# Waiting for each group of eight gathers to land before POOL issues the next

## The reference

```python
x = dense_inputs                                   # [2048, 13]
for W, b, g, be in bot:                            # 13 -> 512 -> 256 -> 64
    x = _bn(relu(x @ W + b), g, be)                # batch norm over the 2048 samples
embs = vmap(lambda tbl, idx: tbl[idx], in_axes=(0, 1), out_axes=1)(emb_tables, sparse_inputs)
T = concatenate([embs, x[:, None, :]], axis=1)     # [2048, 27, 64]
Z = einsum('bnd,bmd->bnm', T, T)                   # all pairs of the 27 vectors of a sample
h = concatenate([x, Z[:, iu, ju]], axis=1)         # 64 + 351 features
for W, b, g, be in top:                            # 415 -> 512 -> 256 -> 1
    h = _bn(relu(h @ W + b), g, be)
return sigmoid(h)
```

## Time and profile before

| | before |
|---|---|
| median of 3 runs | 589.98 us |
| lowest, highest | 588.6, 590.01 us |
| profiled execution, first to last instruction | 987.2 us |
| mean granted PE clock in it | 0.662 of full speed |
| PE, PEld, DVE, ACT, POOL busy | 448.2, 321.1, 233.0, 189.5, 401.1 us |
| gathers: L320, L331 | 390, 26 instructions |
| queue of the gathers | 13312 packets, 13.66 MB, 10.6% of 16 engines |

### The profile page before, as it was taken

One profiled execution on the slowest core, in us unless ns is written; L12 is line 12 of the kernel. 1 busy time (PEld: TensorE's weight loads), 2 busy tenths in 40 slices (PEclk: granted clock), 3 DMA queues, 4 the chain that ended last, 5 costly groups with the idle time before them and its releaser, 6 DMA issues.

```text
span 987.2 us, 13898 instructions
## 1 busy us (share of the span) xinstructions
PE 448.2 (45%) x5827; PEld 321.1 (33%) x5827; DVE 233.0 (24%) x640; ACT 189.5 (19%) x509; POOL 401.1 (41%) x426
## 2 busy tenths in 40 slices
PE   7751151624425161523517162351715244177787
PEld 3430020513214051412405051240514133165664
DVE  6600130402112040312204031220403022055542
ACT  5400020302011030302103030210303021044523
POOL 6777227072542707163361706336171634500000
PEclk9975575756657575755757575575757557577999
DMA  5122001020110202010110101011020101100000
GB/s 168 23 27 26 12 9 26 3 26 10 18 18 11 26 3 27 7 23 14 14 23 5 26 6 23 14 14 23 5 27 6 24 13 15 22 3 1 3 1 0
DMA packets 15895, 18.30 MB, mean 19 GB/s; under 512 B 7614, under 2 KB 8894, under 8 KB 15695
## 3 DMA queue, kind: packets, MB, share of 16 engines
q0 software_dynamic: 13312, 13.66, 10.6%
q1 hardware_dynamic: 2524, 3.72, 1.2%
HBM read 17.34 MB, written 0.01 MB: 18 GB/s over the span
## 4 chain that ended last, share of the span: by engine, by line
another core or an unknown queue 61%; PE 23%; ACT 10%; issue 3%; DVE 3%; DMA 0%; ACTq 0%; SPq 0%; DVEq 0%
PE l_bank L469 11%; ACT Zs L280 7%; PE l_bank L409 3%; PE l_bank L393 2%; PE l_bank L466 2%; PE l_bank L399 1%; PE l_bank L423 1%; ACT TT L636 1%; PE z_bank L455 1%; PE l_bank L507 1%; PE tr_bank L351 1%; DVE TT L853 1%; ACT hidden L582 0%; ACT hidden_hi L648 0%
## 5 line engine op out<-in xcount | busy, mean ns | idle before, releaser
L320 POOL DMA_INDIRECT emb<-table,stage x390 | 374.3, 960 | 424.1 <-DVE stage L802 309.2
L455 PE MATMUL z_bank<-TT 64*27 64x26 f32 x3840 | 127.5, 217 | 403.5 <-issue 388.4
L455 PEld LDWEIGHTS z_bank<-TT 64*27 64x27 f32 x3840 | 89.2, 132 | 442.9 <-issue 442.9
L254 DVE COPY Zs<-z_bank 27x112 f32<-27x112 f32 (+3 forms) x272 | 88.2, 324 | 498.7 <-remote 488.6
L280 ACT ACTIVATE Zs<-z_bank 27x112 f32<-27x112 f32 (+3 forms) x272 | 91.6, 337 | 552.8 <-remote 535.2
L469 PE MATMUL l_bank<-Zs,tw_sb 128*128 128x128 f32 x840 | 117.1, 298 | 0.0
L469 PEld LDWEIGHTS l_bank<-Zs,tw_sb 128*128 128x128 f32 x840 | 112.6, 215 | 0.0
L853 DVE COPY TT<-tr_bank 128x512 f32<-128x512 f32 (+1 forms) x60 | 51.1, 979 | 4.2 <-PE tr_bank L441 3.9
L351 PE MATMUL tr_bank<-idle_operand 128*128 128x512 bf16 x112 | 46.9, 590 | 0.0
L864 DVE BATCH_NORM_STATS2 stats_t<-h_block 128x128 f32 x60 | 17.7, 294 | 123.8 <-ACT hidden_hi L648 123.8
L441 PE MATMUL tr_bank<-ident,emb 128*128 128x128 f32 x195 | 30.8, 284 | 35.1 <-DVE TT L853 28.8
(11 more groups left out here) (120 smaller groups left out, 282.5 us busy)
## 6 DMA issues: line engine op xcount, KB each, us to landing
emb<-table,stage POOLq DMA_INDIRECT x416
tw_sb<-tw0x SPq DMA_DIRECT2D x1, 1792.0 KB
bw_sb<-bw SPq DMA_DIRECT2D x1, 512.0 KB
tw_sb<-tw SPq DMA_DIRECT2D x1, 512.0 KB
twx_sb<-twx SPq DMA_DIRECT2D x1, 256.0 KB
idx_raw<-idx SPq DMA_DIRECT2D x1, 169.0 KB, 3.0
bw_sb<-bw SPq DMA_DIRECT2D x2, 64.0 KB
hidden<-dense_t SPq DMA_DIRECT2D x1, 104.0 KB
```

The costliest lines, as they stand in the source:

```text
L254: last = copy(dst, src[:, :, ZC * q:ZC * q + w])
L320: pool.indirect_dma_start(out=emb[:, s, k, h, :], out_offset=None, in_=table, in_offset=bass.IndirectOffsetOnAxis(ap=stage[:, s, col:col + ...
L455: mm = nc.tensor.matmul(bank[QUAD * j:QUAD * j + V, x * ZM:(x + 1) * ZM], one, one[:, 1:V], start=True, stop=True)
```

## The change

After a group of gathers POOL waits until that group has landed, adds one to a new semaphore that nothing waits for, and then issues the next group. This happens between groups of the same part, so three times in each of parts 0 to 14. The order of the gathers, their tiles and their semaphores stay as they are. There is no wait after the last group of a part, and the gathers of part 15 are unchanged.

```diff
+        group_started = sem("group_started")
...
                     pool.wait_ge(slot_open, it * SLOTS + (s + 1))
                     pool.sem_inc(part_started, 1)
-                    for k in range(TP):
-                        for h in range(2):
-                            col = 2 * k + h
-                            pool.indirect_dma_start(
-                                out=emb[:, s, k, h, :], out_offset=None, in_=table,
-                                in_offset=bass.IndirectOffsetOnAxis(ap=stage[:, s, col:col + 1], axis=0),
-                            ).then_inc(landed[s][k // GROUP], 16)
+                    for g in range(GROUPS):
+                        if g > 0:
+                            pool.wait_ge(landed[s][g - 1], (it + 1) * (len(group_pairs(g - 1)) * 2 * 16))
+                            pool.sem_inc(group_started, 1)
+                        for k in group_pairs(g):
+                            for h in range(2):
+                                col = 2 * k + h
+                                pool.indirect_dma_start(
+                                    out=emb[:, s, k, h, :], out_offset=None, in_=table,
+                                    in_offset=bass.IndirectOffsetOnAxis(ap=stage[:, s, col:col + 1], axis=0),
+                                ).then_inc(landed[s][g], 16)
```

## The result

| | before | changed |
|---|---|---|
| median | 589.29 us | 694.59 us |
| lowest, highest | 588.0, 590.01 us (4 runs) | 694.14, 696.11 us (4 runs) |
| profiled execution, span | 987.2 us | 693.4 us |

The changed kernel is slower by 105.3 us, a ratio of 1.179 (95% interval 1.1773 to 1.1809). The forecast was 676 us with a range of 645 to 704: direction and mechanism hold, and the size of a pause was put too low.

What follows compares the result with a forecast made beforehand. The prediction took POOL's issue of gathers as the bound. Each of 45 pauses adds 1.4 + 0.81 - 0.30 = 1.9 us, 86 us together, so 590 + 86 = 676 us, with a range of 645 to 704.

Steps and rivals of the forecast that it cites:

- The bound: Timed runs are bound by POOL's issue of gathers from 4.5 to 530 us, 32.5 us a part against PE's 21.3.
- a slot open near 85: Without the crawl, the first slot for gathered data would be reopened near 85 us, against 138.98 in the trace.
- POOL is not the bound: Rival: PE sets the 590 us and pauses fill POOL's waits for a slot; time stays or falls to 530; chance 0.05.
- term (a): In each pause between groups, the last gather's data must land: 1.4 us from the end of its instruction.
- Term (b): In each pause, POOL must wake, do the increment and get the next gather going: 0.81 us.
- Term (c): The usual 0.30 us between two gathers is no longer paid by itself, so it comes off each pause.
- The high bound for (a): Landing of a group's last gather takes 1.6 us at the most from the end of its instruction.
- the sum's own high bound: 45 pauses between groups at 1.6 + 0.81 = 2.4 us, with nothing saved: 108 us, 698 us in all.
- The estimate counted from the end of the instruction: By the skill's fixed transfer cost, a pause adds 2.0 + 0.8 - 0.3 = 2.5 us: 113 us, 703 us in all.
- The late semaphores: Rival: packet records end before POOL sees the count; a pause adds 2.8 us, 126 us, 716 us in all; chance 0.07.
- the crawl of PE: PE issues only a few products at a time while POOL gathers; nearly all of it was taken to come from the recording.
- What could give time back: In the bottom network, pauses leave perhaps three fewer gathers lengthened from 0.94 to 1.4 us beside a DVE operation: -1.5 us.

Runs made afterwards that it cites:

- Runs 4 and 6: 4: kernel before with 20 more idle PE multiplies per loop part, 589.55 us; 6: kernel before with two gathers fewer in parts 0 to 14, 551.31 us.
- run 5: The kernel before, unchanged, recorded a second time: 588.51 us, recorded span 586.6 us.
- run 1: The changed kernel with each of its 45 waits and increments moved behind two gathers of the next group: 591.80 us.

## Why the prediction was right, and where it wasn't

**The bound: right.** POOL's issue sets the end. Runs 4 and 6 show it from both sides: 20 more multiplies of PE a part change about 1 us, and 30 fewer gathers give 37.2 us. The model of the chain from a disturbed recording, with the 416th gather at 529.0, a slot open near 85 and a sum of 585.5, is met by the clean recording of run 5: 529.13, 85.5 and a span of 586.6. The rival "POOL is not the bound" needed a gather of 1.07 us or less; it is 1.24.

One detail of that sum was right by luck. I took the chain through the last gather. In run 5 it leaves POOL at the 21st gather of part 15, which completes the first group of the second half:

```profile
522.89 2.72 DMA emb<-table,stage
525.61 0.04 issue
525.65 1.12 PE tr_bank L479 x4
```

PE is then busy until 532.2, when the last gather has landed anyway (530.08 + 1.78 = 531.9). Both paths end within half a microsecond of each other.

**The cost of the waits: right in kind, 0.4 us short in size.** The forecast was 86 us, measured are 105.3. The prediction's own term (a) was mis-sized. It took 1.4 us from the end of the last gather to its landing, read from the transfer engines' activity; measured is 1.78 (2.73 - 0.95). Term (b), 0.81, was measured as 0.79. Term (c), 0.30, is the one seen. The pause is then 1.78 + 0.79 - 0.30 = 2.27 us. 45 of them make 102 us. The other 3 us are pauses that are longer than the rest. The kernel's first stands beside SP's loads, and its landing comes 3.92 us after the gather's start instead of 2.73:

```profile
13.87 3.92 DMA emb<-table,stage
...
387.45 3.41 DMA emb<-table,stage
```

The first line, the kernel's first pause, is worth 1.2 us of the 3. The second line is from the loop, where SP transfers nothing; what makes its landing late isn't shown.

The high bound for (a), 1.6 us "at the most", was passed as well. That the time still lies under the 698 us of the sum's own high bound is in part luck: this bound, 1.6 + 0.81 = 2.4 us a pause, holds only because it doesn't take off the 0.30.

The rule of the Trainium skill on the fixed cost of a transfer (page "DMA: Bandwidth & Descriptors", section "Anatomy of one DMA — SWDGE (gpsimd) path": about 2 us, most of it the receipt of the write) speaks of a wait behind the data. The traces agree in kind, but they show only a quarter of a microsecond between the last recorded activity and the release of POOL, and no run tells whether the recorded activity holds more of it. The measured time is 2.7 us from the start of the gather and 1.78 from its end, and neither is 2.0. The estimate counted from the end of the instruction, 703 us, lies 8 us above the result; my sum lay 19 below.

**The late semaphores: the half of a rival that came true.** It had the count arrive after the packets, with one more idle stretch and no 0.30 taken off, 2.8 us a pause. The count does come late, by 0.25 us and not by 0.4, and the 0.30 does come off: 2.34 us a pause as timed.

**The recording: wrong.** I took the crawl of PE for something that goes with the gathers whenever this program is recorded, and expected a span near 1070 us for the changed kernel, or less if the pauses interrupt the crawl. It was 693.4, and the kernel before had 586.6 in its second recording, with the same gathers. That the crawl wasn't in the timed runs was right, and it is what the sum stood on. What caused it in one recording of eleven stays open; no run here brought it back.

**What could give time back: it did, by about 2 us.** The forecast said -1.5 us, from three fewer lengthened gathers beside the bottom network. In run 5 there are 13 gathers of 1.33 to 1.41 us up to 36 us, each with DVE's operation at L830 starting up to 0.2 us before it. In the changed kernel there are 9, of 1.28 to 1.44 us. All gathers above 1.0 us together are 6.6 us longer than 0.945 us each in run 5, and 4.6 us in the changed kernel. Every one of the 13 stands beside that operation, but no run tests whether the shared port is the reason.

## What to carry to other kernels

Where an engine that only issues transfers is the bound, a wait for its own last transfer puts the latency of a transfer plus the engine's restart, here 2.73 + 0.79 = 3.5 us, in the place of one step of its issue, 1.25 us. The difference of 2.3 us was paid at every wait, behind two gathers as behind eight. If such a wait is needed, look for a place some transfers later: moved two gathers on, the same 45 waits cost 3.3 us instead of 105.3.

When a recording is far longer than the timed runs, look for the chain of steadily spaced instructions that adds up to the timed median, and record again before any idle time in it is priced.

## What the runs showed of the hardware

- A gather of 128 rows of 256 bytes holds POOL for 0.94 us and the next starts 0.30 us later; its semaphore is full 2.7 us after its start (1.78 after its end), whether one or seven gathers of its burst are ahead of it; a few took 3.4 to 3.9 us.
- The count arrives about 0.25 us after the last activity of the transfer engines in the windows of the changed kernel (323.0 and 323.24).
- POOL needs 0.79 us from the landing to the start of the next gather, 0.75 of them after the increment, and 0.07 us for a second increment. Where the landing falls into a running gather (run 1), nothing of this shows.
- One recording of the kernel before had PE's instructions spaced out beside the gathers and a span of 987.2 us for a kernel of 588.5; the second had 586.6. I had not expected the same program to be recorded so differently.
